# Flamingo block: maximum jobs of four heads in even steps, every other job in one PSUM bank, one output bank, later weight jobs

## The reference, cut to what matters

```
x = x + tanh(g_xattn[0]) * mha(layernorm(x), ctx, ctx)        # x (4,512,512), ctx (4,1601,512)
    scores = qh @ kh.T / sqrt(32); causal mask; softmax; @ vh
x = x + tanh(g_ffn[0]) * ffn(layernorm(x))
    qx, sx, sc = fp8 rows of x[:, idx]
    g, u = qlinear(qx, w_gate), qlinear(qx, w_up)             # weights (1408,512)
    t = silu(g) * u
    y = qlinear(fp8 rows of t, w_down)                        # weights (512,1408)
```

## Time and profile before

| | |
|---|---|
| median of three runs | 1158.43 us (1156.97 to 1160.3) |
| profiled execution | 1161.19 us, its span 1159.4 us |
| mean granted clock of TensorE | 0.949 of full speed |
| PE, DVE, ACT, POOL busy in the span | 970.5, 859.7, 656.5, 332.1 us |
| copy of the maxima of groups 1 to 15 (step 23 of the group before) | first at 124.91, last at 986.16 us |

### The profile page before, as it was taken

How to read it: one execution, slowest core, us unless ns; L and a number is a source line. 1 busy time by engine, 2 the same in 40 slices (tenths; PEclk the granted TensorE clock), 3 DMA queues, 4 the chain that set the end, 5 groups by cost and what they waited for, 6 DMA issues and landing times.

```text
span 1159.4 us, 21085 instructions
## 1 busy us (share of the span) xinstructions
PE 970.5 (84%) x7770; PEld 399.4 (34%) x7770; DVE 859.7 (74%) x1438; ACT 656.5 (57%) x1343; POOL 332.1 (29%) x350
## 2 busy tenths in 40 slices
PE   4588889888879989999889999998899999984344
PEld 2233333333323334343334333333333343432222
DVE  7768789887747888777677877787778786446764
ACT  2165567675646666666556666665566666753321
POOL 3012323332101414132323232222314132443343
PEclk9998899999989999999999999999999999996766
DMA  7942423230572221114812121218421110000000
GB/s 147 154 122 69 115 66 93 66 86 26 112 88 57 66 57 39 53 43 83 124 41 60 63 61 36 51 41 115 70 61 35 27 41 10 2 10 10 10 10 19
DMA packets 155119, 70.69 MB, mean 61 GB/s; under 512 B 111032, under 2 KB 142856, under 8 KB 155016
## 3 DMA queue, kind: packets, MB, share of 16 engines
q1 hardware_dynamic: 153256, 63.57, 26.5%
q0 software_dynamic: 1760, 5.77, 1.8%
HBM read 39.08 MB, written 4.19 MB: 37 GB/s over the span
## 4 chain that ended last, share of the span: by engine, by line
PE 42%; DVE 36%; issue 10%; ACT 4%; POOL 4%; DMA 2%; SPq 1%; POOLq 0%; DVEq 0%; ACTq 0%
DVE mch L1069 17%; PE ps L866 13%; PE ps L842 8%; PE ps L887 6%; PE ps L780 5%; PE ps L910 3%; DVE ff L985 2%; DVE ff L981 2%; DVE ff L989 2%; PE ps L785 2%; ACT pr L632 1%; DVE upd L1112 1%; DMA qst<-mrow 1%; PE ps L848 1%; DVE cmb L1102 1%
## 5 line engine op out<-in xcount | busy, mean ns | idle before, releaser
L632 ACT ACTIVATE pr<-ps 128x512 f32<-128x512 f32 (+4 forms) x832 | 397.2, 530 | 250.0 <-PE ps L842 125.1
L1069 DVE TENSOR_REDUCE mch<-ps 128x2 f32<-128x1024 f32 (+4 forms) x416 | 432.3, 1056 | 69.2 <-PE ps L780 32.8
L866 PE MATMUL ps<-pr,vf 128*33 128x512 f32 (+4 forms) x1664 | 380.6, 537 | 0.0
L842 PE MATMUL ps<-qst,kst 97*64 97x512 f16 (+4 forms) x1600 | 250.5, 371 | 18.0 <-DMA qst<-mrow 11.4
L780 PE MATMUL ps<-kTh,qTh 32*128 32x512 f16 (+4 forms) x832 | 156.2, 373 | 59.2 <-DVE mch L1069 40.7
L780 PEld LDWEIGHTS ps<-kTh,qTh 32*128 32x128 f16 x832 | 39.5, 92 | 279.0 <-DVE mch L1069 106.9
L842 PEld LDWEIGHTS ps<-qst,kst 97*64 97x64 f16 (+1 forms) x1600 | 77.3, 111 | 108.0 <-ACT pr L632 57.4
L866 PEld LDWEIGHTS ps<-pr,vf 128*33 128x33 f32 (+1 forms) x1664 | 86.8, 113 | 56.6 <-issue 4.9
L1141 DVE SCALAR_TENSOR_TENSOR ff<-ps,scs,wsb 128x352 f32<-128x352 f32 x56 | 32.6, 583 | 73.1 <-PE ps L887 73.1
L448 POOL TENSOR_TENSOR t_q<-ff 128x768 bf16<-128x768 f32 (+1 forms) x28 | 47.4, 1694 | 100.1 <-DVE ff L989 100.1
L887 PE MATMUL ps<-wgu,t_T 128*64 128x352 bf16 x768 | 66.5, 316 | 0.0
(11 more groups left out here) (151 smaller groups left out, 1198.2 us busy)
## 6 DMA issues: line engine op xcount, KB each, us to landing
kst<-kTh SPq DMA_DIRECT2D x128, 100.1 KB, 2.2
ksrc<-in_ctx SPq DMA_DIRECT2D x16, 768.0 KB
vf<-in_ctx SPq DMA_DIRECT2D x48, 256.0 KB, 5.1
kst<-kTl SPq DMA_DIRECT2D x64, 100.1 KB, 2.2
xs<-in_x SPq DMA_DIRECT2D x16, 256.0 KB, 4.8
qst<-qTh SPq DMA_DIRECT2D x128, 32.0 KB, 1.9
out<-xs SPq DMA_DIRECT2D x16, 256.0 KB, 2.0
ff<-in_L_ffn_w_down SPq DMA_DIRECT2D x4, 704.0 KB, 4.4
```

The lines of the kernel that those rows point to most:

```text
L632: nc.scalar.activation(pr[0:kn, n % NP, q0:S], ps[0:kn, j, q0:S], ACT.Exp, scale=SCALE).then_inc(ex_done, 1)
L842: last = nc.tensor.matmul(ps[a:e, j, q0:S], kst[s][0:ST, r, k0 + a:k0 + e], qst[s][0:ST, r, q0:S], start=True, stop=(t < DT))
L866: nc.tensor.matmul(ps[64 * j:64 * j + VW, 2 + pp % 2, q0:S], vf[0:kn, t, h, :], pr[0:kn, n % NP, q0:S], start=(t == 0), stop=(t == NT - 1) ...
L1069: nc.vector.tensor_reduce(mch[:, qt, 2 * hp:2 * hp + 2, c], both[:, :, 0:k1 - k0], AX.X, ALU.max).then_inc(dve_free, 1)
```

## The change

- A `max` job is one chunk for all four heads of the group, in banks 4 to 7, in every even step; 13 per group. DVE still reduces two heads in an instruction, now two of these per job. For a masked chunk PE writes all four heads before it adds the masks.
- All other jobs use bank 3 alone (keys staged at start-up use banks 4 to 7 as well). Keys are staged in four parts (steps 3, 5, 7, 9), queries in step 15. `up` is split into `gate` and `up`, `hidden` into two `hid` jobs, the large weight jobs into two parts. The tables place most of them one to a step.
- On PE these jobs now stand ahead of the scores of their step, max first; ACT does their copies, and `out_copy`, ahead of the exponentials; DVE takes the turned output first, then the maxima.
- The output of every head pair goes to bank 2: the first values of a pair wait for the copy of the pair before.
- Weight jobs begin 14 steps later. SP's order is not changed.
- Row tiles 0 to 7 lie two steps earlier, 8 to 11 are 22 steps apart; tile 11 ends in step `LAST` + 1, not + 16. In the tail every job has one bank of all eight in turn, and the rounding of the hidden rows stands two steps later.

```diff
-        chunks += full[0:4] + [last[2], last[0], last[1], last[3]] + full[4:]
+    chunks = full[0:2] + [last[0], last[3]] + full[2:7] + [last[1], last[2]] + full[7:]
...
-        return (gg + 1, j) if gg + 1 < GALL else None
+        return (gg + 1, j // 2) if j % 2 == 0 and gg + 1 < GALL else None
-    STAGE_AT, SUMS_AT, SUF_AT, FINISH_AT, MT_AT = {10: 1, 13: 2, 19: 0}, 6, 8, STEPS - AHEAD, 23
+    STAGE_AT, SUMS_AT, SUF_AT, FINISH_AT, MT_AT = {3: 1, 5: 2, 7: 3, 9: 4, 15: 0}, 6, 8, STEPS - AHEAD, 23
...
-    ROWS_AT, UP_AT, HIDDEN_AT, DOWN_AT = 5, (7, 9, 11, 13), 23, 25
+    ROWS_AT, GATE_AT, UP_AT, HIDDEN_AT, DOWN_AT = 5, (6, 8, 12, 14), (7, 9, 13, 15), (23, 24), 26
...
-        return STEPS * (n + NG) + 15 if n < TAIL else LAST + 7 + 13 * (n - TAIL)
+        if n < TAIL - QT:
+            return STEPS * (n + NG) + 13
+        return STEPS * (TAIL - QT + NG) + 13 + 22 * (n - TAIL + QT) if n < TAIL else LAST + 7 + 13 * (n - TAIL)
...
-        return 1 + 7 * j if j < DC else 1 + 7 * DC + 3 * (j - DC)
+        return 15 + (7 * j if j < DC else 7 * DC + 3 * (j - DC))
...
-            banks[job] = 4 + 2 * (len(banks) % 2)
+        banks[job] = (next(ALL_BANKS),) if tail else at
...
+    def numbered_max(gg, j):
+        for hp in range(PAIRS):
+            numbered("max", gg, j, hp, at=(4 + 2 * hp, 5 + 2 * hp))
...
+            for r in range(GH):
+                if r % 2 == 0:
+                    free_slot(pe, ("max", gg, j, r // 2))
+                rows = slice(HD * r, HD * r + HD)
+                last = nc.tensor.matmul(ps[:, 4 + r, 0:k1 - k0], qTh[rows, gg % 2, qt * P:(qt + 1) * P],
                                         kTh[rows, gg % 2, k0:k1], start=True, stop=(hi <= lo))
+                if r % 2 == 1 and hi <= lo:
+                    last.then_inc(mx_mm, 1)
...
-            if t == 0 and pp >= 2:
-                pe.wait_ge(o_ev, pp - 1)
+            if t == 0 and pp >= 1:
+                pe.wait_ge(o_ev, pp)
...
+            for hp in range(PAIRS):
+                dve.wait_ge(mx_mm, PAIRS * (gg * CH + j) + hp + 1)
+                nc.vector.tensor_reduce(mch[:, qt, 2 * hp:2 * hp + 2, c], ps[:, 4 + 2 * hp:6 + 2 * hp, 0:k1 - k0],
+                                        AX.X, ALU.max).then_inc(dve_free, 1)
```

More of the change, by code:

```diff
@@ L47, in flamingo_gated_block @@
     SPB = NG * STEPS
-    K_CUT = 8 * P
     HALVES = ((0, P // 2), (P // 2, P))
     assert IT * P == I and DT + QT == NT - 1
[L52 to L59, removed]
-        chunks += full[0:4] + [last[2], last[0], last[1], last[3]] + full[4:]
+    full, last = [], []
+    for qt in range(QT):
+        end = NEAR + P * (qt + 1)
+        for c in range((end + 511) // 512):
+            k0, k1 = 512 * c, min(512 * c + 512, end)
+            (full if k1 - k0 == 512 else last).append((qt, c, k0, k1))
+    chunks = full[0:2] + [last[0], last[3]] + full[2:7] + [last[1], last[2]] + full[7:]
     CH = len(chunks)
-    assert CH == STEPS
+    assert 2 * CH == STEPS
     AHEAD = 6
@@ L116, in flamingo_gated_block @@
     banks, before_in_bank, latest, dve_count, act_count = {}, {}, {}, {}, {}
[L118 to L121, removed]
-            banks[job] = 4 + 2 * (len(banks) % 2)
-        before_in_bank[job] = latest.get(banks[job])
-        latest[banks[job]] = job
-        if job[0] not in ("weight", "shift", "rows", "hidden") and not (job[0] == "up" and job[1] >= TAIL):
+    ALL_BANKS = itertools.cycle(range(8))
@@ L126, in numbered @@
+    def numbered(*job, at=(3,)):
+        kind, n = job[0:2]
+        tail = kind in ("rows", "gate", "up", "hid", "down") and n >= TAIL
+        banks[job] = (next(ALL_BANKS),) if tail else at
+        before_in_bank[job] = [latest[b] for b in banks[job] if b in latest]
+        for b in banks[job]:
+            latest[b] = job
+        if kind in ("stage", "max", "suf", "turn", "gate", "down"):
             dve_count[job] = len(dve_count) + 1
-        if job[0] in ("weight", "shift", "rows", "hidden") or job[0] == "up" and job[1] < TILES - QT:
+        elif not (kind == "up" and tail):
@@ L137, in flamingo_gated_block @@
-    for j in range(AHEAD):
-        numbered("max", 1, j)
+    numbered_stage(1)
+    for j in range(AHEAD // 2):
+        numbered_max(1, j)
     for at in range(END):
         gg, u = divmod(at, STEPS)
+        if turned_at(at) is not None:
+            numbered("turn", turned_at(at))
+        if max_job_at(at) is not None:
+            numbered_max(*max_job_at(at))
         if gg + 2 < GALL and u in STAGE_AT:
             numbered("stage", gg + 2, STAGE_AT[u])
-        if turned_at(at) is not None:
-            numbered("turn", turned_at(at))
```

330 lines of the change are left out of this document (167 added, 163 removed).

## The result

The changed kernel takes 1243.2 us (1238.2 to 1250.1, 4 runs) where the kernel before, on the same chip, takes 1157.7: a ratio of 1.074 (95% interval 1.069 to 1.080). It is slower by 7.4%; 1138 was forecast. Its profiled execution took 1243.66 us, with a span of 1241.9.

The account below looks back on a forecast made before the run. The prediction took PE to bound the attention, with 13 us of DVE slack in a tile group. Its terms, -31 + 3 + 21 + 3 + 0 - 16 = -20 us, took 1158.4 to 1138 us; range 1120 to 1155.

Parts of the forecast that it names:

- The max jobs: Four heads run side by side on PE, saving 0.38 us a job (0.32 to 0.44), 192 jobs: 73 us if nothing else held PE.
- What DVE and bank 3 give back: Waits return 5.4 of 4.9 + 5.4 terms: 51.6 + 5.4 = 57.0 us a group, 1.8 at `rows`; eleven groups, -31 us.
- The count for steps 4 to 10: Some 18 us of DVE against 16 of PE in these steps; 3 us (1 to 5) of PE waits put on it.
- Weight jobs: They only move; 1.5 us gained in four groups (-6), turns ahead of the scores +9: together +3 us (-10 to +15).
- SP at step 26: Block 3's load waits for POOL, maxima queue behind it: PE waits 17 us, low clock after; +21 us (15 to 27), once.
- Rival D: No stall at step 26, because block 1 is ready sooner: 1117 us, chance 0.03.
- Start-up and batch changes: Masked start-up jobs hand over heads later, less 1 us for staged keys: +3 us (0 to 5); batch changes 0 (-6 to +6).
- The tail: Tile 11 moved into the attention saves 14 us against 5.6 there, plus 8 for later tiles: -16 us (-4 to -24).
- the 8 us for tiles 13 to 15: In the tail, rows 14 and 15 are rounded earlier and a gate job passes them: 2.7 us each, 8 together (0 to 12).
- A: DVE doesn't hold PE back; a group gains 4.5 instead of 2.8 us: 1112 us, chance 0.2.
- B: Four strips don't run as two do, or DVE takes it all: 1158 us, chance 0.17.
- C: Bank 3 is the bound: jobs ahead of the scores wait 0.4 us each for its readers: 1171 us, chance 0.18.

Follow-up runs that it names:

- experiment 8: The changed kernel with maxima for two heads per step and reductions of only the first 64 columns (part of the work left out): 1197.2 us, against 1156 with four heads.
- experiment 6: The changed kernel with maxima made for two heads in even and two in odd steps, everything else as changed: 1245.2 us.
- experiment 11: The changed kernel with the four edits of experiment 10, but maxima made for two heads per step: 1167.4 us.
- experiment 2: The changed kernel with POOL's rounding of a tile's rows ahead of the addition of the turned output: 1200.9 us.
- experiment 4: The changed kernel with only the weight jobs behind scores and values on PE, and their copies behind the exponentials on ACT: 1225.9 us.
- experiment 5: The changed kernel with weight jobs starting in step 1 again, not step 15: 1248.8 us.
- experiment 7: The changed kernel with each reduction of maxima reading only the first 64 columns of its banks, the rest of that DVE work left out: 1156.4 us.
- the repair: The changed kernel with SP issuing the load of weight block 3 behind the copy of the maxima of group 1: 1227.9 us.
- experiment 9: The changed kernel with tiles 8 to 11 spaced 26 steps apart again, not 22, so tile 11 ends behind the attention: 1233.0 us.
- experiment 3: The changed kernel with tile and weight jobs behind scores and values on PE, and their copies behind the exponentials on ACT: 1207.7 us.
- the best version: Experiment 10's kernel plus two edits of DVE's order: rounding of rows ahead of the maxima, staged key parts in steps 3, 6, 9, 12: 1154.0 us, ratio 0.9936.
- experiment 10: The changed kernel with four edits together, those of the repair, experiment 2, experiment 4 and experiment 9: 1165.9 us, ratio 1.0043.

## Why the prediction was wrong

20 us less were forecast, 85 more came. The steps that failed most are the price of `rows` in the attention, the price of tile 11 there, and a saving of the max jobs that was taken off in full. By stretches, distances 5 to 12 are 45 us over the forecast (8 x 2.8 us less forecast, 23.0 more measured), and what follows them is over it by about as much again.

**The max jobs** (-73 us on PE). The mechanism is right, four strips run at once. The size is not: 0.30 us per job was measured with DVE out of the way (experiment 8), against 0.38 taken and a lower bound of 0.32. That is 57 us, not 73. Read off the pair's start to the scores, 0.32 us, the worth of a full job was right; the step that failed is the 0.06 added from the comparison of two full steps, for a turn from values to max and back that the odd steps would save. The saving stands at the lower end, not at the upper. And in the kernel as changed nothing of it came out (experiment 6); with the four edits it is 1.2 us of an ordinary distance and nothing over the whole (experiment 11).

**What DVE and bank 3 give back** (5.4 us a group, distance 57.0). Measured 62.1. Two things were left out. (a) "Step 16 has a double maximum ahead of the rounding of rows, then POOL's 1.3": this leaves out POOL's own order. The addition of the turned output stands in front, waits for the join, and adds 1.9 us to the wait, which is 3.4 us and not 1.8. (b) The low clock after the wait was counted for the stall at step 26 and forgotten here, although it comes back in eleven groups. The 1.9 us of (a) with their part of (b) are 3.4 us of an ordinary distance and 42 us of the whole (experiment 2), the most that any edit of the order took back.

The count for steps 4 to 10 held: 18 us of DVE, and 16 of PE with 3 of waits. These seven steps take 19.3 us (810.57 to 829.86), DVE busy for 17.1. Before they took 17.1 (757.59 to 774.73; not quite the same jobs). So the 3 us that were put back are about what the stretch took: the saving of its four jobs, some 1.3 us, does not come out (experiment 6), and 2.2 us come on top. With (a), (b) and the job size (4.9 - 3.8 = 1.1 us) this makes up nearly all of the 5.1 us between 57.0 and 62.1, as an estimate, since the job size was measured with short reductions.

**Weight jobs** (+3). Measured: the turns ahead of the scores cost 12 to 17 us (experiment 4), for 9 counted, and the "1.5 in four groups" gained from maxima isn't seen. The step "they only move" was wrong as well: the move by itself is worth 20 us (experiment 5), which the forecast didn't have at all. The sum, without the stall, is 346.0 - 331.0 = +15 us for distances 0 to 4. With the move worth -20 and the turns 12 to 17, some 18 to 23 us are left that no run assigns; the maxima on DVE are the nearest cause, since short reductions gave back 22 us there (experiment 7).

**SP at step 26** (+21, wait 17). The mechanism is right: the wait is 16.3 us, the slow clock follows, and the repair gave 15 us in the median and 16.7 in the span. That is the wait alone; the 3 us counted for the clock behind it were not got back. Rival D is out.

**Start-up and batch changes** (+3 and 0). Right in size: +2.9 us; distances 8 and 12 grew by 3.7 and 2.4 where ordinary ones grew by 2.3.

**The tail** (-16). Measured, from distance 13 to the end: 18.4 + 14.8 - 8.4 = +24.8 us. The work of tile 11 behind the attention was 9.6 us and not 14, and inside it costs 16.5 and not 5.6 (experiment 9): the step that failed is pricing it there by PE's busy time alone. That tiles 9 to 11, 22 steps apart, now meet maxima and staging in other steps than the table was made for is the likely reason; which meeting costs what was not traced. Rows of tile 12 are measured 7.5 us after the join of the last turned output, as the forecast had it, not 12.7:

```profile
1129.75 0.23 DVE L1121 TENSOR_TENSOR den<-cw,ps 128x4 f32<-128x4 f32 x2 [0.65 <-PE ps L840]
...
1137.25 0.69 DVE L1144 TENSOR_REDUCE scs<-vf 128x1 f32<-128x512 f32 x1 [0.88 <-ACT vf L654]
```

But the 8 us for tiles 13 to 15 were not there: with tile 11 back in the tail it takes 122.3 us where it took 121.1, and from the `rows` of tile 14 to those of tile 15 it is 23.3 us (1161.74 to 1185.08) where it was 22.7 (1085.78 to 1108.51). The rounding of rows 14 passes the hidden rows of tile 12, but these pay for it: their halves are turned 3.96 us apart, those of tile 15 2.81. In between DVE scales a gate chunk (0.58 us), and its first pass over the second half takes 1.83 us beside POOL's subtraction. For tile 15 the first pass takes 0.48 us and the second 1.97 (last rows), so the slow pass by itself is not the difference; the account of it is open:

```profile
1163.08 1.81 POOL L461 TENSOR_TENSOR pr<-kst 128x768 bf16<-128x768 f32 x1 [1.49 <-DVE kst L1010]
1163.41 1.83 DVE L1002 TENSOR_SCALAR kst<-kst 128x640 int32<-128x640 int32 x1
...
1165.03 0.80 PE L914 MATMUL ps<-idb,pr 128*128 128x128 bf16 x6 [1.40 <-POOL pr L461]
...
1168.99 0.69 PE L914 MATMUL ps<-idb,pr 128*128 128x128 bf16 x5 [3.15 <-POOL pr L461]
...
1226.99 0.48 DVE L1002 TENSOR_SCALAR ff<-ff 128x640 int32<-128x640 int32 x1
...
1227.51 1.97 DVE L1006 TENSOR_SCALAR ff<-ff 128x640 f32<-128x640 f32 x1
```

**The rivals.** A is out. B's first half is false (strips), its second, "DVE takes it all", is what experiment 6 shows, but at 1158 us it left out everything else. C had the sign and the mechanism only in part: jobs ahead of the scores do cost, but in the weight groups and at batch changes; in ordinary groups moving them behind changed nothing (experiment 3). Its wait for bank 3 behind DVE is there all the same, 2.1 us in steps 4 to 10 (rows in experiment 6). Whether a second bank would take it away was not tried, so C is not refuted as to the bank. The Trainium skill's rule (TensorEngine Tiling, PSUM Bottleneck: after four-way tiling the emptying of PSUM may be the bound) was set aside because DVE's total was below PE's; that totals decide was the prediction's reading and is not in the rule. Experiments 6 and 7 agree with the rule (87 us less with short reductions): not the total over a group decides but the stretches in which DVE has hardly a gap.

**What stays open.** Which wait costs the batch changes 9 us each, clock included, when the tile jobs stand ahead; what the 18 to 23 us in distances 0 to 4 are; whether bank 3 or DVE's pace holds steps 4 to 10; which part of the 12 us each of DVE's two edits gave; and 4.9 us in the last group, which takes 57.0 us to the last turned output even in the best version, for 52.1 before.

## What to carry to other kernels

A saving on the engine that is busiest counts only in stretches in which it does not wait for another one that has no gap; lay the stretches side by side before you multiply by the number of jobs. Where a job is moved in front of the critical work, follow what it waits for through *every* queue, with the order of the last engine in its own step: two instructions on a POOL that was idle three quarters of the time cost 42 us here. Price a wait with the clock after it, and as often as it comes.

## What the runs showed of the hardware

How much a short wait costs depends on whether the clock falls after it, and that was not to be read from the wait's length alone. After 1.54 us of wait for the `rows` job the granted clock stayed at 1.00 in one kernel (experiment 10's, first row), after 1.53 us it fell in another (experiment 2's, at the job of 570.87 us, second row): the distance that holds this job takes 60.3 us, its neighbour, with the same wait and the clock at 1.00, 58.7; after 1.75 us it fell as far as after 3.37 (short reductions, third row; changed kernel, fourth). Each window holds the 4 us from the `rows` job on.

```profile
547.30:551.30 4.00, 3.98 (x34) 1.64 (x36) 3.48 (x7) 2.66 (x5) 0.73 (x1) 1.00 0.50 76
```

```profile
570.80:574.80 4.00, 3.93 (x24) 1.89 (x26) 2.90 (x4) 1.57 (x3) 0.72 (x1) 0.64 0.64 63
```

```profile
710.90:714.90 4.00, 3.96 (x22) 1.74 (x24) 0.00 (x0) 1.66 (x3) 0.00 (x0) 0.57 0.31 74
```

```profile
847.50:851.50 4.00, 3.97 (x22) 1.75 (x24) 0.26 (x1) 1.66 (x3) 0.00 (x0) 0.57 0.02 4
```
